# A tuned float32 block kernel on one Trainium2 core: the last down projection as seven block products

## The reference

```
x = x + 0.5 * ffn(layernorm(x))                 # all float32
x = x + mix(layernorm(x))                       # z = x W^T, gated scan over time, layernorm
x = x + 0.5 * ffn(layernorm(x))
ffn(x) = (silu(x @ w_gate.T) * (x @ w_up.T)) @ w_down.T
```

## Time and profile before

| | |
|---|---|
| three runs | 1021.63, 1021.67, 1021.70 us |
| span of the profiled execution | 1020.2 us |
| TensorE busy | 1014.4 us, 99% |
| VectorE, ScalarE, GpSimd busy | 66%, 40%, 16% |
| matmuls | 4508 |
| DMA | 218 MB, 214 GB/s over the span |

### The profile page before, as it was taken

How to read it: one execution, slowest core, us unless ns; L and a number is a source line. 1 busy time by engine, 2 the same in 40 slices (tenths; PEclk the granted TensorE clock), 3 DMA queues, 4 the chain that set the end, 5 groups by cost and what they waited for, 6 DMA issues and landing times.

```text
span 1020.2 us, 12550 instructions
## 1 busy us (share of the span) xinstructions
PE 1014.4 (99%) x4508; PEld 841.2 (82%) x4508; DVE 671.5 (66%) x1013; ACT 408.6 (40%) x669; POOL 162.5 (16%) x187
## 2 busy tenths in 40 slices
PE   8999999999999999999999999999999999999998
PEld 8888888888888888888888888888888888888887
DVE  7756665598988687857978877786685333333342
ACT  6645446465433622224732363231382322222311
POOL 4123343125300200210430020021040000000000
PEclk9999999999999999999999999999999999999999
DMA  6588877678667555647856764454677565555265
GB/s 206 224 325 318 301 265 253 252 229 272 242 227 231 182 181 167 200 144 236 270 167 230 235 216 150 146 185 141 228 252 225 207 191 193 204 196 190 85 189 187
DMA packets 61710, 217.89 MB, mean 214 GB/s; under 512 B 6352, under 2 KB 15568, under 8 KB 53968
## 3 DMA queue, kind: packets, MB, share of 16 engines
q1 hardware_dynamic: 61072, 216.03, 62.8%
q10 hardware_dynamic: 576, 1.05, 0.3%
HBM read 170.92 MB, written 46.14 MB: 213 GB/s over the span
## 4 chain that ended last, share of the span: by engine, by line
PE 99%; DVE 1%; DMA 0%; POOL 0%; ACT 0%; issue 0%; DVEq 0%; ACTq 0%
PE ps_a L1569 8%; PE ps_a L1571 8%; PE ps_a L1570 8%; PE ps_b L1569 8%; PE ps_b L1571 8%; PE ps_b L1570 8%; PE ps_c L1569 7%; PE ps_c L1571 7%; PE ps_c L1570 7%; PE ps_d L1569 7%; PE ps_d L1571 7%; PE ps_d L1570 7%; PE aux L1569 3%; PE aux L1571 3%; PE aux L1570 3%; PE ps_d L1731 1%
## 5 line engine op out<-in xcount | busy, mean ns | idle before, releaser
L1060 DVE TENSOR_TENSOR tmp<-tmp,ps_c 128x512 f32<-128x512 f32 x59 | 40.4, 685 | 138.9 <-PE ps_c L1571 138.9
L1569 PE MATMUL ps_a<-xt,gu 128*128 128x512 f32 x304 | 118.3, 389 | 0.0
L1570 PE MATMUL ps_a<-xt,gu 128*128 128x512 f32 x304 | 118.3, 389 | 0.0
L1571 PE MATMUL ps_a<-xt,gu 128*128 128x512 f32 x304 | 118.3, 389 | 0.0
L1570 PE MATMUL ps_b<-xt,gu 128*128 128x512 f32 x286 | 111.3, 389 | 0.0
L1571 PE MATMUL ps_b<-xt,gu 128*128 128x512 f32 x286 | 111.3, 389 | 0.0
L1569 PE MATMUL ps_b<-xt,gu 128*128 128x512 f32 x286 | 111.3, 389 | 0.0
L1571 PE MATMUL ps_d<-dn,hid 128*128 128x512 f32 x256 | 99.6, 389 | 0.0
L1569 PE MATMUL ps_d<-dn,hid 128*128 128x512 f32 x256 | 99.6, 389 | 0.0
L1570 PE MATMUL ps_d<-dn,hid 128*128 128x512 f32 x256 | 99.6, 389 | 0.0
L1570 PE MATMUL ps_c<-xt,gu 128*128 128x512 f32 x236 | 91.8, 389 | 0.0
(11 more groups left out here) (207 smaller groups left out, 2113.7 us busy)
## 6 DMA issues: line engine op xcount, KB each, us to landing
dn<-dn_kept SPq DMA_DIRECT2D x112, 512.0 KB, 3.7
gu<-gu_kept SPq DMA_DIRECT2D x46, 1024.0 KB, 5.0
gu<-gu_kept SPq DMA_DIRECT2D x46, 768.0 KB, 5.6
gu_kept<-gu SPq DMA_DIRECT2D x14, 1024.0 KB, 4.4
gu_kept<-gu SPq DMA_DIRECT2D x14, 768.0 KB, 4.2
dn_kept<-dn SPq DMA_DIRECT2D x16, 512.0 KB, 5.1
h_t<-w_ffn_in SPq DMA_DIRECT2D x18, 256.0 KB, 4.8
x_tok<-w_ffn_in SPq DMA_DIRECT2D x18, 256.0 KB, 5.1
```

What stands on the lines that cost most here:

```text
L1060: dve.tensor_tensor(dst, u3s(si), p5_bank(si)[:, :], ALU.add).then_inc(c22_done, 1)
L1569: pe.matmul(dst, a_hi, b_hi, start=start, stop=False, skip_group_check=chained)
L1570: pe.matmul(dst, a_hi, b_lo, start=False, stop=False, skip_group_check=chained)
L1571: return pe.matmul(dst, a_lo, b_hi, start=False, stop=stop, skip_group_check=chained)
```

## The change

In phase 3 the down projection of both token tiles is no longer two products but seven block products, for a 2 by 2 scheme: token tile (2 or 3) by half of the output (left or right 256 columns), and even by odd hidden tiles within a pair.

- **Phase 0.** For each pair of hidden tiles GpSimd makes four sums of down weight blocks (`t_sums_of`: four operations of 128x256), ScalarE and VectorE split them (`t_hi_of`, `t_lo_of`: 128x1024 each) in the rows 2, 3 of both parts of `zx`, and SP stores them in `t_kept` (`keep_t`: two DMAs of 512 KB in pieces of 1 KB, after `keep_dn` of the same set). This is done in even sets, for the last pair (pair 7) in set 15. `load_dn_raw` also waits for `t_sums`. The window's first two `d1_hi` wait for the last `t_lo`, the third and fourth for the last store.
- **Phase 3, in the sets.** After `prod6` stands `first_block` (12 matmuls of 256 columns), nothing after `prod4`. With it the first two of the seven products are made into `x_ps` and `y_ps` (the four banks `ps_d`). The results for the first token tile are written to free rows (`first_row`) and kept. GpSimd forms four sums of 128x512 per pair (`s_of`).
- **Phase 3, after the sets.** `first_block` for pair 7 twice, then 20 batches (`batch`): the products Q5, Q6, Q3, Q7, Q4 of four batches each, a batch being 24 matmuls of 256 columns. ScalarE (`stage_hi_of`) and VectorE (`stage_lo_of`) split 128x1024 for each into one of seven slots of `xt`; `fetch_dn` brings the weights from `t_kept` or `dn_kept`, four buffers as before. `add_product` adds half of a product to a block of the output. Q7 and Q4 use the same banks: the first batch of Q4 waits for `block_added` 12.
- Tile 2 goes out in one DMA after its last addition, tile 3 in a right half and two pieces of the left half.

```diff
+        t_kept = nc.dram_tensor("t_kept", [PAIRS, P, 4, 2, HALF], F32).ap()
...
+        x_ps, y_ps, z_ps = [ps_d[0], ps_d[1]], [ps_d[2], ps_d[3]], [aux, ps_a]
...
+        def by_half(row):
+            return row.rearrange("p (a n) -> p a n", a=2)
+
+        def t_raw(j):
+            r = 4 * (j % 2)
+            return zx_rows[:, r:r + 2, :].rearrange("p r (a n) -> p (r a) n", a=2)
+
+        def t_part(part):
+            return zx[:, part, 2:4, :].rearrange("p r (a n) -> p (r a) n", a=2)
+
+        def first_rows(i, odd):
+
+            if i == 0:
+                return h_t[:, 2 * odd:2 * odd + 2, :]
+            if i == 1:
+                return zw[:, :, :].bitcast(F32) if odd else gb[:, :, :]
+            r = 4 * odd + 2 * (i - 2)
+            return x_tok[:, r:r + 2, :]
+
+        def first_row(q, odd):
+            return first_rows(q // 2, odd)[:, q % 2, :]
+
+        def stage_rows(w, i):
+
+            return {Q5: hid1[:, 4 * i:4 * i + 3:2, :], Q6: zx_rows[:, 2 * i:2 * i + 2, :], Q3: first_rows(i, 1),
+                    Q7: first_rows(i, 0), Q4: hid1[:, 4 * i + 1:4 * i + 4:2, :]}[w]
+
+        def stage_op(n):
+            return STAGES[n % len(STAGES)]
...
+            def keep_t(j):
+                sp.wait_ge(t_lo, j + 1)
+                for part in range(2):
+                    sp.dma_start(t_kept[j, :, :, part], t_part(part).bitcast(F32)).then_inc(t_stored, 16)
...
+                if n < SEG + DN:
+                    sp.wait_ge(d_done, n - DN + 1)
+                elif n < SEG + PAIRS + DN:
+                    sp.wait_ge(first_done, 2 * (n - SEG - DN + 1))
+                else:
+                    sp.wait_ge(batch_done, n - SEG - PAIRS - DN + 1)
+                if n < SEG:
+                    kept = dn_kept[n % HT]
+                elif n < SEG + PAIRS:
+
+                    q = n - SEG
+                    kept = dn_kept[2 * q:2 * q + 2, :, 0].rearrange("h p t n -> p h t n")
+                else:
+                    w, i = divmod(n - SEG - PAIRS, 4)
+                    if n == SEG + PAIRS:
+                        sp.wait_ge(t_stored, 32 * PAIRS)
+                    if w == Q3:
+                        kept = dn_kept[4 * i + 1:4 * i + 4:2, :, 1].rearrange("h p t n -> p h t n")
+                    else:
+                        c = {Q5: 0, Q7: 1, Q6: 2, Q4: 3}[w]
+                        kept = t_kept[2 * i:2 * i + 2, :, c].rearrange("j p t n -> p j t n")
+                sp.dma_start(dn[:, n % DN, :, :, :].bitcast(F32), kept).then_inc(dn_loaded[n % DN], 16)
 
...
+            def t_hi_of(j):
+                act.wait_ge(t_sums, 4 * j + 4)
+                if j == 0:
+                    act.wait_ge(plain_done, 8)
+                wait(act, t_stored, 32 * j)
+                act.copy(t_part(0), t_raw(j)).then_inc(t_hi, 1)
...
             def d1_hi(p, m):
                 wait(act, d_done, 32 * p + 16 + m - 4 + 1 if m >= 4 else 32 * p)
-                if m < 4 and p == 0:
-                    act.wait_ge(plain_done, 8)
+                if m < 2 and p == 0:
+                    act.wait_ge(t_lo, PAIRS)
+                if 2 <= m < 4 and p == 0:
+                    act.wait_ge(t_stored, 32 * PAIRS)
                 if m < 4 and p in (1, 2):
...
+            def stage_hi_of(n):
+                w, i = divmod(n, 4)
+                if n < len(STAGES):
+                    done = {B11: p1_done, B21: p2_done, T2: p6_done, T3: p7_done, T1: p5_done, T4: p4_done,
+                            B22: p3_done}[stage_op(n)]
+                    act.wait_ge(done, upto(SETS * PH - 1))
+                else:
+                    act.wait_ge(batch_done, n - len(STAGES) + 1)
+                act.wait_ge(s_step, 4 * (2 * i + 1) + (2 if w == Q5 else 4))
+                act.copy(xt[:, stage_op(n), 0, :, :], stage_rows(w, i)).then_inc(stage_hi, 1)
...
+            def t_sums_of(j):
+
+                even, odd = dn_raw[:, 0, :], dn_raw[:, 1, :]
+                b11, b12, b21, b22 = even[:, 0:HALF], even[:, HALF:D], odd[:, 0:HALF], odd[:, HALF:D]
+                t = t_raw(j)
+                pool.wait_ge(dn_raw_arrived[0], 16 * (j + 1))
+                pool.wait_ge(dn_raw_arrived[1], 16 * (j + 1))
+                wait(pool, t_lo, j - 1)
+                pool.tensor_tensor(t[:, 0, :], b12, b11, ALU.subtract).then_inc(t_sums, 1)
+                pool.tensor_tensor(t[:, 1, :], b22, b12, ALU.subtract).then_inc(t_sums, 1)
+                pool.wait_ge(t_sums, 4 * j + 1)
+                pool.tensor_tensor(t[:, 2, :], b22, t[:, 0, :], ALU.subtract).then_inc(t_sums, 1)
+                pool.wait_ge(t_sums, 4 * j + 3)
+                pool.tensor_tensor(t[:, 3, :], b21, t[:, 2, :], ALU.subtract).then_inc(t_sums, 1)
+
+            def s_of(q):
+
+                tile1_even, tile1_odd = hid1[:, 2 * q, :], hid1[:, 2 * q + 1, :]
+                s3, s4, s2 = first_row(q, 0), first_row(q, 1), zx_rows[:, q, :]
+                pool.wait_ge(hid1_done, 16 * LAST + 2 * q + 2)
+                pool.wait_ge(lo0_ready, 16 * LAST + 2 * q + 2)
+                pool.tensor_tensor(s3, first_row(q, 0), tile1_even, ALU.subtract).then_inc(s_step, 1)
+                pool.wait_ge(s_step, 4 * q + 1)
+                pool.tensor_tensor(tile1_even, tile1_even, tile1_odd, ALU.add).then_inc(s_step, 1)
+                pool.tensor_tensor(s2, tile1_odd, s3, ALU.subtract).then_inc(s_step, 1)
+                pool.wait_ge(s_step, 4 * q + 3)
+                pool.tensor_tensor(s4, first_row(q, 1), s2, ALU.subtract).then_inc(s_step, 1)
...
+            def t_lo_of(j):
+                dve.wait_ge(t_hi, j + 1)
+                dve.tensor_tensor(t_part(1), t_raw(j), t_part(0).bitcast(F32), ALU.subtract).then_inc(t_lo, 1)
+
+            def stage_lo_of(n):
+                w, i = divmod(n, 4)
+                dve.wait_ge(stage_hi, n + 1)
+                dve.tensor_tensor(xt[:, stage_op(n), 1, :, :], stage_rows(w, i),
+                                  xt[:, stage_op(n), 0, :, :].bitcast(F32), ALU.subtract).then_inc(stage_lo, 1)
+
+            def add_block(banks, b, tile, half, semaphore, n, added=0):
+
+                dve.wait_ge(semaphore, n)
+                wait(dve, block_added, added)
+                x = x_tok[:, 4 * tile + 2 * b:4 * tile + 2 * b + 2, half * HALF:(half + 1) * HALF]
+                dve.scalar_tensor_tensor(x, by_half(banks[b][:, :]), 0.5, x, ALU.mult, ALU.add
+                                         ).then_inc(block_added, 1)
+
+            def add_product(w):
+
+                banks, tile, half, added = {Q5: (z_ps, 3, 1, 0), Q6: (x_ps, 2, 1, 0), Q3: (z_ps, 2, 1, 8),
+                                            Q7: (x_ps, 3, 1, 6), Q4: (x_ps, 3, 0, 0)}[w]
+                add_block(banks, 0, tile, half, bank_done, w + 1, added)
+                add_block(banks, 1, tile, half, batch_done, 4 * w + 4, added)
 
             def zw_lo_of(j):
                 dve.wait_ge(zw_hi, j + 1)
...
+            stage_lo_of(1)
+            stage_lo_of(2)
+            for b in range(2):
+                add_block(x_ps, b, 2, 0, first_done, 2 * PAIRS - 1)
+            stage_lo_of(3)
+            for b in range(2):
+                add_block(y_ps, b, 2, 0, first_done, 2 * PAIRS, b + 1)
+            stage_lo_of(4)
+            for n in range(5, 20):
+                stage_lo_of(n)
+                if n % 4 == 1:
+                    add_product(n // 4 - 1)
+            add_product(Q4)
...
+            def unit_half(banks, t):
+                return banks[t // 2][:, t % 2 * HALF:(t % 2 + 1) * HALF]
+
+            def first_block(q, odd):
+
+                n = SEG + q
+                if odd == 0:
+                    pe.wait_ge(dn_loaded[n % DN], 16 * dn_loads(n))
+                pe.wait_ge(lo0_ready, 16 * LAST + 2 * q + odd + 1)
+                if q == 0 and odd == 0:
+                    pe.wait_ge(hid21_done, 8 * LAST + 1)
+                    pe.wait_ge(c11_done, upto(SETS * LAST + 1))
+                if q == 0 and odd == 1:
+                    pe.wait_ge(c12_done, upto(SETS * LAST + 1))
+                for t in range(ST):
+                    a = slice(t * P, (t + 1) * P)
+                    last = three(unit_half(y_ps if odd else x_ps, t), hid0[:, odd, 0, a], hid0[:, odd, 1, a],
+                                 dn[:, n % DN, odd, 0, :], dn[:, n % DN, odd, 1, :], q == 0 and t % 2 == 0,
+                                 q == PAIRS - 1, True)
+                last.then_inc(first_done, 1)
+
+            def batch(w, i):
+                m = 4 * w + i
+                n = SEG + PAIRS + m
+                banks = z_ps if w in (Q5, Q3) else x_ps
+                pe.wait_ge(dn_loaded[n % DN], 16 * dn_loads(n))
+                pe.wait_ge(stage_lo, m + 1)
+                if i == 0 and w == Q5:
+                    pe.wait_ge(y1_added, 4 * LAST)
+                    pe.wait_ge(c11_done, upto(SETS * PH - 1))
+                if i == 0 and w != Q5:
+
+                    pe.wait_ge(block_added, {Q6: 2, Q3: 6, Q7: 8, Q4: 12}[w])
```

(25 more changed lines are left out.)

116 lines of the change are left out of this document (89 added, 27 removed).

## The result

The changed kernel takes 1024.78 us (median of five runs, 1023.68 to 1027.28), the kernel before, run beside it, 1021.63 (1021.58 to 1021.70). The ratio is 1.0032, with a 95% interval of 1.0021 to 1.0044: slower by 3.15 us, where 2.0 us faster was forecast. The profiled execution took 1024.07 us with a span of 1022.0, and is one of the quicker ones.

A forecast was written before the change was run, and what follows sets the result against it. TensorE, busy 99%, was taken to bound the kernel; -6.4 + 3.0 + 0.1 + 0.3 + 0.9 + 0.1 = -2.0 us gave a span of 1018.2 and a time of 1019.7 us, range 1016.0 to 1022.1.

The forecast's parts named there:

- What bounds it: Whole kernel: TensorE, busy 99%, sets the time by its number of matmuls times their spacing, plus a tail.
- Terms on TensorE: Last phase's down projection: 672 matmuls of 256 columns at 120 ns replace 384 of 512, gaining 6.4 us.
- The zero for the sums in phase 0, before its end: Even sets of phase 0: added GpSimd, ScalarE and VectorE work is covered and costs zero.
- The end of phase 0: Set 15 and the window after: pair 7's last store lands late and delays VectorE's subtractions, 3.0 us lost.
- TensorE is late only once: End of phase 0: the 0.5 us wait for hidden tile 15 is part of the 3.0 us lost.
- (c): Before the last product: TensorE waits until VectorE has read the product before from the same banks, 0.9 us.
- (a): Second half of pair 7 after the last set: TensorE waits for VectorE's low half, 0.1 us (0 to 0.2).
- (b): Fourth batch after the last set: operands need two GpSimd operations on pair 7, 0.3 us (0 to 1.1).
- the fifth rival: First batches after the last set: five products repeatedly wait for operands, about 2 us more, 1021.7; chance 0.10.
- the fourth (D): ScalarE's wait for pair 7: stores in 1 KB pieces land late, 1024.9 at a landing of 10.4 us; chance 0.08.
- The range: Whole kernel: from 1016.0, taking in B, to 1022.1, the forecast with a late landing of 7.6 us.
- The time outside the span: Around the profiled span: the median of the runs lies 1.5 us above it.

The follow-up runs named there:

- four edits of order: Changed kernel with stores one set earlier, pair 7 earlier, last product's wait bank by bank, first sums earlier: 1017.91 us, ratio 0.9962 to the kernel before.

## Why the prediction was wrong

- **What bounds it:** right. TensorE alone sets the time, and every us gained or lost is a spacing or a gap of its own.
- **Terms on TensorE:** right, 6.5 us for 6.4.
- **The zero for the sums in phase 0, before its end:** this step failed, 2.5 us. It counted the durations of the new operations, not what they wait for and what they hold up. Two places were missed or taken as covered. ScalarE's copy for a pair waits until the pair before has been stored; SP issues that store behind a 1024 KB load, and the copy stands ahead of ScalarE's release of a bank. The prediction itself had the landing of 7.6 us for such a load in the earlier trace rows and did not put it in front of this store. It cost 1.7 us. The other place is GpSimd's 2.9 us at 22 us. The prediction saw it, gave it 2.4 us of cover from the earlier trace rows up to 34.87, and named "up to 1 us" if that went. The weights of set 2 did come in time (33.6 us, wanted at 34.55); but the chain of VectorE operations runs on without a gap to the release of ps_a at 43 us, and there the cover was smaller. It cost 0.8 us.
- **The end of phase 0:** the mechanism was right, step by step: ScalarE waiting for the store, VectorE's window shifted, the later gap ended by its subtractions into zx. The size was 4.2 us for 3.0: the last store landed 6.1 us after the end of the subtraction, where 5.2 were taken (0.6 to the second issue, 5.5 to its landing), which made VectorE 4.6 us late instead of 3.85; and behind every wait TensorE lost 0.08 us more, five times in that window. The claim that TensorE is late only once held.
- **After the last set:** (c) 1.1 us for 0.9, right. (a) 0.2 us for 0.1, at the place and by the operation that it named: VectorE's low half ends at 957.61 + 0.69 = 958.30, TensorE goes on at 958.35. (b) cost nothing. Its 5 to 9 us do not come out of its own rows: two operations of 1.29 to 1.75 us with 1.05 and 1.22 behind them are 4.9 to 5.8 us, and the fifth rival's 9 us fall with them. Measured from the first GpSimd operation to the end of VectorE's subtraction it was 960.84 to 967.69, 6.9 us, since the two took 2.2 us each; the fourth batch wanted it at 968.5. So GpSimd's elementwise work, against which the Trainium skill advises (GPSIMD Engine Reference, section Engine selection), did no harm there; the harm was at the start, where it met VectorE.
- **Rivals.** The nearest is the fourth (D), by its sign and because a store landed late with ScalarE waiting for it. But it looked at pair 7, where the landing took 5.5 us and not 9.3 or more; the late one, 9.8 us, was at pair 0. And its cause, pieces of 1 KB, made about 1 us of that landing; the place behind the load of x made the larger part, 9.8 us against 5.2 ahead of it. The fifth, repeated waits for operands, did not occur.
- **Spread.** No term for it was in the prediction. The range ended at 1022.1 because landings were varied at one place only. The time outside the span was taken as 1.5 us and was 1.8 to 2.1 us.

## What to carry to other kernels

Where one engine is busy 99% of the time, cost every new instruction by what it waits for and by what stands behind it in its queue, not by its duration: here waits at five places, 0.7 to 3.5 us each, ate a saving of 6.5 us, and four edits of order, with no less work, gave 6.9 us back. For a store that someone waits for, look at what is issued ahead of it on the same queue. Where a buffer is filled again each turn, as zx here, look at whether its store can be issued in the turn in which it is filled: at pair 0 that was worth 1.95 us.

## What was not expected of the hardware

A gap may cost more than its length. In the profiled execution of the version with the first sums earlier TensorE waited at 76 us as above, and then, 1.1 us after it had gone on, its clock fell. TensorE's timeline, and the granted clock by stretch (us; PE busy, PEld, DVE, ACT, POOL; PEclk; DMA share; GB/s):

```profile
76.42 0.50 PE L1783 MATMUL ps_b<-xt,gu 128*128 128x512 f32 x1 [1.84 <-ACT tmp L680]
...
77.50 0.63 PE L1784 MATMUL ps_b<-xt,gu 128*128 128x512 f32 x1
77.93 0.63 PE L1785 MATMUL ps_b<-xt,gu 128*128 128x512 f32 x1
...
80.88 0.40 PE L1783 MATMUL ps_b<-xt,gu 128*128 128x512 f32 x1
```

```profile
77.00:81.00 4.00, 4.00 (x12) 3.13 (x11) 3.17 (x5) 2.07 (x4) 0.55 (x1) 0.57 1.05 401
81.00:95.00 14.00, 14.00 (x64) 11.53 (x63) 8.28 (x12) 5.84 (x10) 4.18 (x6) 1.00 0.75 277
```

Eight times in a row the matmuls of 512 columns stand about 427 ns apart instead of 227 (1.2 GHz instead of 2.4), which costs eight times 0.2, 1.6 us. In the changed kernel's profiled execution the same gap was 0.45 us shorter and the clock stayed; in that of the version with pair 7 sooner it was 0.2 us shorter (1.63 us by the same measure), and the clock stayed too. That the gap brought the clock down is a reading from one execution, not shown by a run of its own. The slowest of the changed kernel's five runs, 1027.28 us, has a mean clock of 0.998, as has the execution above, where its profiled one has 1.000; so the same is likely to have happened there, though no timeline of that run shows it. Of all executions six list 0.998, and all six are of versions whose first store of sums stands behind the load of x.

A second thing: in the version with only VectorE's low part moved, pair 7's stores were issued 0.8 us sooner and landed nearly when they had landed before, since they were slower by 0.7 us. Why isn't shown; a fetch stands behind them in both.
